# Spreading the steps of two routings and one channel attention over the slots of a hand-planned order, in a three-layer float32 network kernel

## The chip, the cores and the metric

The kernel runs on one NeuronCore of a Trainium2 chip, in one launch. The metric is the device time of that launch in microseconds (us); less is better. Names of engines: PE is TensorE (matrix products), DVE is VectorE, ACT is ScalarE, POOL is GpSimd, SP is SyncE, which starts the transfers.

## What is computed

`x` is 4 batches of 512 tokens with 128 features, in float32. Four layers follow, each adding to `x`, each behind a layer norm:

```
x = x + channel_attention(layernorm(x))   # "A": RMS norm, q k v, 8 heads, softmax(q k^T) over channels
x = x + moe_ffn(layernorm(x))             # "F": router softmax over 8 experts, a small net picks how many
x = x + token_attention(layernorm(x))     # "B": 512x512 scores, banded multipliers, softmax
x = x + moe_ffn(layernorm(x))             # "F" again, the same weights

def moe_ffn(h):
    probs = softmax(h @ router.T)                                  # 8 experts
    k     = argmax(gelu(h @ w1.T + b1) @ w2.T + b2) + 1            # 1 to 6
    score = where(rank(probs) < k, probs, 0)
    return sum_e score[e] * (silu(h @ gate[e].T) * (h @ up[e].T)) @ down[e].T
```

All eight experts are computed for all tokens; the score multiplies their hidden values.

## The kernel before, in words

**Chunks and slots.** The hidden units of the 8 experts (8 x 336) lie as 21 chunks of 128. A feed-forward layer over one batch of 512 tokens is a block of 21 chunks; there are 4 batches and 2 such layers, so 8 blocks and 168 chunks, numbered k = 0 to 167. One slot of the plan is one chunk. In each slot PE makes the gate and the up product of chunk k. Each is three matmuls of 128x512 (a high and a low part of both operands, `three`, L1112 to L1114), into PSUM banks of which gate and up have two each: gate k waits for the silu of chunk k-2, up k waits for DVE's product of chunk k-2. ACT makes `silu` of the gate (L758, step `gu`). DVE multiplies the up bank with it, or with the broadcast scores `sbc` (L1053, step `uk`). POOL multiplies the missing factor in (L635, step `um`). PE then makes the down product from SBUF (step `down`, L1297, two instructions in plain float32). From chunk 121 on, a down may be split like gate and up: ACT writes a high part (`ah`, L768), DVE a low part (`al`, L1061), and PE runs three matmuls in place of the plain product. In the first three blocks `um` multiplies by `sbc`, so a block's ums and downs can't start before its routing is done. 16 buffers `t2` lie between `uk` and `down`.

**Everything else is fitted in between.** The other layers and the routing of each block are chains of steps. Step lists (`A1_STEPS`, `F0_STEPS`, `F1_STEPS`, `F_STEPS`, `B_STEPS`, L88 to L105) give each step a due slot counted from the start of its chain; `A_STARTS` and `B_STARTS` give starts. `plan()` walks the slots. In each it puts first `gu` and `uk`, then the halves `ah`/`al` (`halves`), then up to two ums and downs (`products`), then the due steps of the chains, in a fixed order of chains. A step whose inputs are not yet planned moves its whole chain one slot later; a chain may also be moved once because the costs in `COST` would overfill ACT or DVE in that slot. Last come, every third slot, two `pieces`: ACT copies and POOL differences that split the next gate and up weights into high and low parts (L729, L619). Each engine then executes its part of this one list strictly in order, so that list is the schedule, and all waits between engines are semaphores.

**The steps of a routing.** `stats` (DVE), `rstd` (POOL, a power, L578), `xn` (ACT, four instructions, L655), `xT` (PE transposes, ACT copy to `xhF`), `xl` (DVE, low part, L907), `route` (PE, ACT), `inner` 0 and 1 (POOL, L604 and L607), `rt` (PE, DVE), `rexp` (ACT Exp, L732), `rsum` (DVE: sum, reciprocal, `pr` L1002, and the two comparisons `gt` L1006 and `ge` L1007 of each probability with the 7 others), `rrank` (DVE: `ge` times a triangle L1011, the maximum with `gt` L1013, the sum L1014), `tanh` (ACT), `gelu` (DVE L1019), `act` (PE, 8 small matmuls, L1233), `actk` (DVE, seven small instructions, L1027 to L1037), `sx` (POOL, L600), `sbc` (PE transposes L1241, ACT copy).

**The steps of a channel attention.** `asim` (PE), `ass` (DVE), `apow` (POOL L590), `ascale` (DVE: `qn`, `simT`, L940 and L941), `asT` (PE transpose L1180), `amax` (DVE L950, L953), `aexp` (ACT Exp L706), `awo` (DVE L961, L963), `am`, `am2` (PE and ACT), `y` (PE; DVE adds to X). The token attention has `bs` (PE scores), `bsp` (DVE, the bands, L1071 to L1088), `bexp` (ACT Exp L788), `bpT` (PE transposes L1327), `bo`, `bw`, `byx`.

Exp and Silu need different activation tables on ACT; each change shows as an ACT_TABLE_LOAD.

Of the kernel before, what the change touches and what calls it, by code (L numbers as in the profile page):

```python
# [56 lines left out]
WCH = 3  # L57
# [29 lines left out]
           (11, "asT"), (12, "amax"), (13, "aexp"), (14, "awo"), (16, "am"), (17, "am2"), (19, "y")]  # L87
A1_STEPS = [(2, "asim"), (3, "ass"), (3, "apow"), (4, "ascale"), (7, "asT"), (7, "amax"), (8, "aexp"), (9, "awo"),  # L88
            (11, "am"), (12, "am2"), (14, "y")]
F0_STEPS = [(0, "route"), (1, "inner", 0), (1, "rt"), (2, "rexp"), (3, "inner", 1), (4, "rsum"), (5, "rrank"), (5, "tanh"),  # L90
            (6, "gelu"), (8, "act"), (8, "actk"), (9, "sx"), (11, "sbc")]
F1_STEPS = [(0, "stats"), (0, "rstd"), (0, "xn"), (3, "xT"), (4, "xl"), (6, "route"), (7, "inner", 0), (8, "rt"), (9, "rexp"),
            (9, "inner", 1), (9, "rsum"), (11, "rrank"), (11, "tanh"), (11, "gelu"), (13, "act"),
            (13, "actk"), (14, "sx"), (16, "sbc")]
ROUTED_LATE = (0, 1, 2)
# [7 lines left out]
F_STEPS = [(0, "stats"), (1, "rstd"), (2, "xn"), (4, "xT"), (5, "xl"), (6, "route"), (7, "inner", 0), (8, "rt"), (9, "rexp"),  # L103
           (10, "inner", 1), (11, "rsum"), (12, "rrank"), (12, "tanh"), (13, "gelu"), (15, "act"),
           (15, "actk"), (16, "sx"), (18, "sbc")]  # L105
A_STARTS = (6, 24)
B_STARTS = (29, 48, 67, 90)
# [10 lines left out]
FREED_BY = dict(asim="ascale", asT="amax", act="actk")  # L118

POOL_COST = dict(wp=1.2, wd=1.2, wc=1.5, um=1.4, rstd=1.4, apow=.8, bqkl=1.4, sx=1.1, inner=1)  # L120
COST = dict(stats=(0, 0, 1.2), xn=(0, 1.2, 0), xT=(.4, .5, 0), xl=(0, 0, .6), ag=(.9, .3, 0), ar=(.5, .4, .4),
            asim=(.7, 0, 0), ass=(0, 0, .1), ascale=(0, 0, .3), asT=(.1, 0, 0), amax=(0, 0, .5), aexp=(0, 3, 0),
            awo=(0, 0, .5), am=(.3, .3, 0), am2=(.3, .3, 0), y=(.9, 0, .6), route=(.7, 1.1, 0), rt=(.4, 0, .4), rexp=(0, 2.7, 0),
            rsum=(0, 0, 1.3), rrank=(0, 0, 1.1), tanh=(0, .5, 0), gelu=(0, 0, .6), act=(.9, 0, 0), actk=(0, 0, 1.3),
            sbc=(.4, .5, 0), yT=(.4, 0, .6), bqk=(.7, 1, 0), bs=(.7, 0, 0), bsp=(0, 0, 1.2),
# [3 lines left out]
COST |= dict(ah=(0, .6, 0), al=(0, 0, .9))  # L129
DVE_LOAD = dict(uk=.7, al=.9, stats=1.4, xl=.7, ar=.6, ascale=.5, amax=.6, awo=.5, y=.7, yT=.7, rt=.8, rsum=3.6, rrank=2.9,  # L130
                gelu=1.7, actk=1.6, bv=.7, bsp=1.2, byx=2.4)
# [40 lines left out]
def plan():  # L172
# [12 lines left out]
    debt = [0.0, 0.0]  # L185
    pool_free = [0.0]
    um_end, downs, block_end = [], [0], []
    split, seen = [], [0]
    dve_load = [0.0]
    slot_of = {}  # L190
# [85 lines left out]
    while k < last - 1:  # L276
        n = (k + 1) // CH
        if (k + 1) % CH or (("xl", "F", n) if n in ROUTED_LATE else ("sbc", n)) in done:
            k += 1
            add(("gu", k))  # L280
            assert k < NT2 or ("down", k - NT2) in done
            add(("uk", k))
        else:
            for th in threads:
                th[0] -= th[0] <= k
        halves(k)
        products(k, 2)
        if wds and k >= WD_FROM and k % 2:
            add(wds.pop(0))
            debt[0] += 0.5  # L290
        pe = 2.2
        act, dve = debt[0] + 0.6, debt[1] + 0.7
        for th in threads:
            while th[1] and th[0] + th[1][0][0] <= k:
                s = th[1][0][1]
                cost = COST.get(s[0], (0, 0, 0))
                room = pe + cost[0] + DEBT
                late = (th[2] < SHIFTS
                        and (act + cost[1] > room + (cost[1] > 2) * 3 or dve + cost[2] > room))
                if not ready(s) or late:  # L300
                    th[0] += 1
                    th[2] += 1
                    break
                th[1].pop(0)
                add(s)
                pe, act, dve = pe + cost[0], act + cost[1], dve + cost[2]
        if pieces and k % WCH == 0:
            add(pieces.pop(0))
            add(pieces.pop(0))
        debt = [max(0.0, act - pe), max(0.0, dve - pe)]  # L310
        dve_load[0] = max(0.0, dve_load[0] - pe)
# [11 lines left out]
def build(nc, x_d, small_d, gate_d, up_d, down_d, w2_d, cols_d, rows_d, out_d):  # L323
# [17 lines left out]
    with ExitStack() as ctx:  # L341
# [487 lines left out]
        def _(dve):  # L829
# [16 lines left out]
            for s in steps:  # L846
# [148 lines left out]
                if kind == "rsum":  # L995
# [6 lines left out]
                    chain(dve.tensor_tensor(pr[:, :, :], pe_[:, :, :], p4[:, 2].unsqueeze(2).to_broadcast([P, NT, E]), ALU.mult))  # L1002

                    other = pr[:, :, :].unsqueeze(2).to_broadcast([P, NT, E, E])
# [3 lines left out]
                if kind == "rrank":  # L1008
                    n = s[1]
                    dve.wait_ge(pr_ready, n + 1)  # L1010
                    chain(dve.tensor_tensor(ge[:, :, :, :], ge[:, :, :, :],  # L1011
                                            tri[:, :, :].unsqueeze(1).to_broadcast([P, NT, E, E]), ALU.mult))
                    chain(dve.tensor_tensor(gt[:, :, :, :], gt[:, :, :, :], ge[:, :, :, :], ALU.max))  # L1013
                    chain(dve.tensor_reduce(rk[:, :, :], gt[:, :, :, :], AX_X, ALU.add))  # L1014
# [406 lines left out]
```

## Time and profile before

| | us |
|---|---|
| median of 3 runs | 498.91 (497.41 to 499.11) |
| the profiled execution | 500.59 |
| its span, first to last instruction | 498.5 |
| PE busy | 480.8 (96%) |
| DVE busy | 310.0 (62%) |
| ACT busy | 262.7 (53%) |
| POOL busy | 311.1 (62%) |
| mean granted TensorE clock | 0.990 |

The page divides the span in 40 slices and gives each engine's busy share there, and the clock that TensorE was granted. Beside it, the trace was asked for the waits of PE by stretch, for the timeline of single engines, and for sums over chosen windows. In a timeline, a number in square brackets is how long the engine had been idle before that instruction, and what ended it.

### The profile page before, as it was taken

What the parts mean: (1) busy time and instruction counts of PE and PEld (TensorE: products, weight loads), DVE (VectorE), ACT (ScalarE), POOL (GpSimd) and SP (SyncE); (2) the same over time, 40 slices, a digit from 0 to 9 for tenths busy, and PEclk for the clock granted to TensorE, in tenths of its full rate; (3) what the DMA queues carried; (4) which work ended last, traced back from release to release, by engine and by line L of the source; (5) the groups of instructions that cost most, each with busy time, mean ns of one, the idle gap of its engine ahead of it and who ended that gap; (6) DMA issues with size and microseconds to landing.
All of it is one profiled execution on the core that took longest, in us unless ns stands there. A gap on an engine that the chain in (4) does not pass through costs nothing.

```text
span 498.5 us, 6470 instructions
## 1 busy us (share of the span) xinstructions
PE 480.8 (96%) x2036; PEld 343.5 (69%) x2036; DVE 310.0 (62%) x723; ACT 262.7 (53%) x477; POOL 311.1 (62%) x314
## 2 busy tenths in 40 slices
PE   7898889999999897999999999999999999999997
PEld 7776756677666565576676666667666767778886
DVE  3655434735867746288855984659766466748563
ACT  3495635656714684228762559334773456345551
POOL 5365788429868284445653555557675677759774
PEclk9998899999999998999999999999999999999999
DMA  8700000000000000000000000000000000000000
GB/s 238 239 0 2 0 0 2 0 1 1 1 1 1 1 0 0 1 1 2 0 1 0 1 1 1 1 0 1 22 0 1 1 14 9 0 1 0 24 0 21
DMA packets 7933, 7.36 MB, mean 15 GB/s; under 512 B 732, under 2 KB 7772, under 8 KB 7900
## 3 DMA queue, kind: packets, MB, share of 16 engines
q1 hardware_dynamic: 7900, 6.96, 4.6%
q8 instruction: 16, 0.26, 0.2%
q14 instruction: 17, 0.14, 0.1%
HBM read 5.91 MB, written 1.05 MB: 14 GB/s over the span
## 4 chain that ended last, share of the span: by engine, by line
PE 76%; ACT 3%; DVE 2%; issue 2%; POOL 1%; ACTq 0%; POOLq 0%; DVEq 0%
PE bank L1297 19%; PE bank L1112 16%; PE bank L1114 15%; PE bank L1113 15%; PE bank L1335 3%; PE bank L1233 1%; POOL t L635 1%; PE bank L1327 1%; ACT L758 1%; PE bank L1135 1%; PE bank L1347 1%; DVE t L1053 1%; PE bank L1305 1%; PE bank L1241 1%; PE bank L1275 1%
## 5 line engine op out<-in xcount | busy, mean ns | idle before, releaser
L635 POOL TENSOR_TENSOR t<-t,sl 128x512 f32<-128x512 f32 x105 | 148.5, 1418 | 98.0 <-DVE t L1053 81.0
L758 ACT ACTIVATE sl<-bank 128x512 f32<-128x512 f32 x168 | 99.4, 596 | 135.4 <-PE bank L1114 127.1
L1297 PE MATMUL bank<-t,WD 128*128 128x512 f32 x262 | 130.3, 595 | 0.0
L1053 DVE TENSOR_TENSOR t<-bank,sbc 128x512 f32<-128x512 f32 x105 | 72.3, 689 | 64.8 <-PE bank L1114 63.4
L635 POOL TENSOR_TENSOR t<-t,sbc 128x512 f32<-128x512 f32 x63 | 80.9, 1313 | 20.0 <-DVE t L1053 11.1
L1112 PE MATMUL bank<-xhF,WGh 128*128 128x512 f32 x167 | 90.3, 541 | 1.6 <-ACT sl L758 1.6
L1053 DVE TENSOR_TENSOR t<-bank,sl 128x512 f32<-128x512 f32 x63 | 43.1, 685 | 66.4 <-PE bank L1114 27.7
L1112 PE MATMUL bank<-xhF,WUh 128*128 128x512 f32 x168 | 67.3, 401 | 1.7 <-DVE t L1053 1.7
L1114 PE MATMUL bank<-xhF,WUl 128*128 128x512 f32 x168 | 67.1, 400 | 0.0
L1113 PE MATMUL bank<-xlF,WUh 128*128 128x512 f32 x168 | 67.0, 399 | 0.0
L1114 PE MATMUL bank<-xhF,WGl 128*128 128x512 f32 x167 | 66.7, 399 | 0.0
L1113 PE MATMUL bank<-xlF,WGh 128*128 128x512 f32 x167 | 66.4, 398 | 0.0
L1297 PEld LDWEIGHTS bank<-t,WD 128*128 128x128 f32 x262 | 49.7, 190 | 21.9 <-issue 11.5
L1112 PEld LDWEIGHTS bank<-xhF,WGh 128*128 128x128 f32 x167 | 31.9, 191 | 17.4 <-issue 11.0
L1113 PEld LDWEIGHTS bank<-xlF,WGh 128*128 128x128 f32 x167 | 31.9, 191 | 14.2 <-issue 11.3
L1112 PEld LDWEIGHTS bank<-xhF,WUh 128*128 128x128 f32 x168 | 32.0, 190 | 10.3 <-DVE t L1053 2.8
L1114 PEld LDWEIGHTS bank<-xhF,WUl 128*128 128x128 f32 x168 | 32.0, 190 | 7.7
L1113 PEld LDWEIGHTS bank<-xlF,WUh 128*128 128x128 f32 x168 | 32.0, 190 | 7.5
L1114 PEld LDWEIGHTS bank<-xhF,WGl 128*128 128x128 f32 x167 | 31.7, 190 | 7.5
L758 ACT ACT_TABLE_LOAD x19 | 24.4, 1283 | 0.3
L1061 DVE TENSOR_TENSOR t2r<-t,ah 128x512 fp32r<-128x512 f32 x33 | 23.8, 722 | 0.0
L768 ACT ACTIVATE ah<-t 128x512 fp32r<-128x512 f32 x33 | 20.6, 624 | 3.3 <-POOL t L635 2.4
(209 smaller groups left out, 700.7 us busy)
## 6 DMA issues: line engine op xcount, KB each, us to landing
stage<-in_gate SPq DMA_DIRECT2D x7, 192.0 KB, 6.2
stage<-in_up SPq DMA_DIRECT2D x7, 192.0 KB, 6.3
WD<-in_down SPq DMA_DIRECT2D x7, 192.0 KB, 6.2
X<-in_x SPq DMA_DIRECT2D x4, 256.0 KB, 5.8
out<-X SPq DMA_DIRECT2D x3, 256.0 KB, 2.3
raw<-in_small SPq DMA_DIRECT2D x1, 384.0 KB, 4.9
out<-X SPq DMA_DIRECT2D x2, 128.0 KB, 1.9
raw<-in_small SPq DMA_DIRECT2D x1, 192.0 KB, 2.6
```

The costliest lines, as they stand in the source:

```text
L635: pool.tensor_tensor(t2[k % NT2][:, :], t2[k % NT2][:, :], by[:, :], ALU.mult).then_inc(a_done, 1)
L758: act.activation(sl[k % NSL][:, :], bank[k % 2][:, :], ACT.Silu).then_inc(silu_done, 1)
L768: act.activation(ah[i % NAH][:, :], t2[k % NT2][:, :], ACT.Copy).then_inc(ah_done, 1)
L1053: dve.tensor_tensor(t2[k % NT2][:, :], bank[2 + k % 2][:, :], by[:, :], ALU.mult).then_inc(t2_done, 1)
L1061: dve.tensor_tensor(t2r[k % NT2][:, :], t2[k % NT2][:, :], ah[i % NAH][:, :].bitcast(F32), ALU.subtract).then_inc(al_done, 1)
L1112: pe.matmul(out, lh, rh, start=start, stop=False)
L1113: pe.matmul(out, lh, rl, start=False, stop=False)
L1114: return pe.matmul(out, ll, rh, start=False, stop=stop)
L1135: r = pe.transpose(to[:, i * P:i * P + P], xn[:, i, :], ident[:, :])
L1233: r = pe.matmul(m[:, 8 * i:8 * i + KMAX], hq[:, i * P:i * P + P], w2[:, 0:KMAX], start=True, stop=True)
L1297: r = pe.matmul(OACC[:, :], WD[:, c, :], t2[k % NT2][:, :], start=(c == 0), stop=(c == CH - 1 or k == TAIL[0] - 1))
L1335: r = pe.matmul(m[:, :], xnB[b % 2][:, j, :], PT[:, j, :], start=(j == 0), stop=(j == NT - 1))
```

## The change

Only the order of instructions changes: the same instructions run on the same data.

- `F0_STEPS`, `F1_STEPS` and `A1_STEPS` get new due slots. The first routing's last step `sbc` is due in slot 8 in place of 11, the second's 13 slots after its chain's start in place of 16, the second batch's channel attention ends in slot 11 in place of 14. Most steps stand one slot apart.
- `rsum` is cut in two planned steps, `rsum` (softmax) and `rcmp` (the two comparisons); `rrank` too, into `rrank` (the product with the triangle) and `rmax` (maximum and sum). `F_STEPS` places the four in slots 11, 12, 13, 14.
- The third batch's channel attention starts in slot 7 in place of 6.
- Steps in `AHEAD` (`rstd`, `apow`, `sx`, `xl`, `ascale`, `amax`) that come next in their chain and are due are put right behind `gu` and `uk` of the slot, ahead of the halves, the ums and the downs and of other chains' steps.
- The two pieces that fell every third slot may wait for a slot in which ACT has room by the planner's costs.

```diff
-A1_STEPS = [(2, "asim"), (3, "ass"), (3, "apow"), (4, "ascale"), (7, "asT"), (7, "amax"), (8, "aexp"), (9, "awo"),
-            (11, "am"), (12, "am2"), (14, "y")]
-F0_STEPS = [(0, "route"), (1, "inner", 0), (1, "rt"), (2, "rexp"), (3, "inner", 1), (4, "rsum"), (5, "rrank"), (5, "tanh"),
-            (6, "gelu"), (8, "act"), (8, "actk"), (9, "sx"), (11, "sbc")]
-F1_STEPS = [(0, "stats"), (0, "rstd"), (0, "xn"), (3, "xT"), (4, "xl"), (6, "route"), (7, "inner", 0), (8, "rt"), (9, "rexp"),
-            (9, "inner", 1), (9, "rsum"), (11, "rrank"), (11, "tanh"), (11, "gelu"), (13, "act"),
-            (13, "actk"), (14, "sx"), (16, "sbc")]
+A1_STEPS = [(1, "asim"), (2, "ass"), (3, "apow"), (4, "ascale"), (5, "asT"), (6, "amax"), (7, "aexp"), (8, "awo"),
+            (9, "am"), (10, "am2"), (11, "y")]
+F0_STEPS = [(0, "route"), (1, "inner", 0), (1, "rt"), (2, "rexp"), (2, "inner", 1), (3, "rsum"), (3, "tanh"), (4, "rcmp"),
+            (4, "gelu"), (5, "rrank"), (5, "act"), (6, "rmax"), (6, "actk"), (7, "sx"), (8, "sbc")]
+F1_STEPS = [(0, "stats"), (1, "rstd"), (2, "xn"), (3, "xT"), (4, "xl"), (5, "route"), (6, "inner", 0), (6, "rt"), (7, "rexp"),
+            (7, "inner", 1), (8, "rsum"), (8, "tanh"), (9, "rcmp"), (9, "gelu"), (10, "rrank"), (10, "act"), (11, "rmax"),
+            (11, "actk"), (12, "sx"), (13, "sbc")]
...
-           (10, "inner", 1), (11, "rsum"), (12, "rrank"), (12, "tanh"), (13, "gelu"), (15, "act"),
+           (10, "inner", 1), (11, "rsum"), (12, "tanh"), (12, "rcmp"), (13, "gelu"), (13, "rrank"), (14, "rmax"), (15, "act"),
...
-A_STARTS = (6, 24)
+A_STARTS = (7, 24)
...
+AHEAD = ("rstd", "apow", "sx", "xl", "ascale", "amax")
...
-            rsum=(0, 0, 1.3), rrank=(0, 0, 1.1), tanh=(0, .5, 0), gelu=(0, 0, .6), act=(.9, 0, 0), actk=(0, 0, 1.3),
+            rsum=(0, 0, .9), rcmp=(0, 0, 1.2), rrank=(0, 0, .5), rmax=(0, 0, 1.2), tanh=(0, .5, 0), gelu=(0, 0, .6), act=(.9, 0, 0), actk=(0, 0, 1.3),
...
+        for th in threads:
+            while th[1] and th[0] + th[1][0][0] <= k and th[1][0][1][0] in AHEAD and ready(th[1][0][1]):
+                s = th[1].pop(0)[1]
+                add(s)
+                debt[0] += COST.get(s[0], (0, 0, 0))[1]
+                debt[1] += COST.get(s[0], (0, 0, 0))[2]
         halves(k)
         products(k, 2)
...
-        if pieces and k % WCH == 0:
+        owed += 2 * (k % WCH == 0)
+        while pieces and owed and act < pe + 0.8:
             add(pieces.pop(0))
-            add(pieces.pop(0))
+            owed -= 1
+            act += 0.5
...
-
+                if kind == "rcmp":
                     other = pr[:, :, :].unsqueeze(2).to_broadcast([P, NT, E, E])
                     own = pr[:, :, :].unsqueeze(3).to_broadcast([P, NT, E, E])
...
+                if kind == "rmax":
                     chain(dve.tensor_tensor(gt[:, :, :, :], gt[:, :, :, :], ge[:, :, :, :], ALU.max))
```

## Rows read from the trace of the kernel before

**Rows 1.** The page: shares of the chain that ended last, by engine.
```profile
PE 76%; ACT 3%; DVE 2%; issue 2%; POOL 1%; ACTq 0%; POOLq 0%; DVEq 0%
```

**Rows 2.** PE's waits from 36 to 75 us: us in total, times, longest.
```profile
PE bank L1112 <- DVE t L1053: 1.7, 2, 1.4
PE bank L1112 <- ACT sl L758: 1.6, 1, 1.6
PE bank L1180 <- DVE simT L941: 1.0, 1, 1.0
PE bank L1135 <- ACT xn L655: 0.4, 1, 0.4
...
```

**Rows 3.** PE's waits from 160 to 200 us.
```profile
PE bank L1327 <- DVE xlS L907: 2.5, 1, 2.5
PE bank L1112 <- DVE xlF L907: 1.6, 1, 1.6
PE bank L1112 <- DVE bmp L1085: 0.5, 1, 0.5
```

**Rows 4.** PE's waits from 300 to 412 us.
```profile
PE bank L1135 <- ACT PT L796: 0.5, 1, 0.5
PE bank L1135 <- ACT xn L655: 0.3, 1, 0.3
...
```

**Rows 5.** Windows: stretch, length, busy us of each engine, granted clock, DMA.
```profile
42.00:44.00 2.00, 2.00 (x7) 1.52 (x6) 1.76 (x10) 0.60 (x1) 1.82 (x4) 0.50 0.00 0
75.00:160.00 85.00, 85.00 (x352) 58.66 (x351) 53.50 (x133) 45.14 (x81) 59.12 (x60) 1.00 0.00 1
191.00:198.00 7.00, 4.48 (x14) 2.86 (x14) 4.22 (x7) 1.79 (x3) 3.46 (x3) 0.76 0.00 0
```

**Rows 6.** Timeline of DVE, 33 to 45 us: start, us, instruction, idle before.
```profile
35.40 0.68 DVE L1053 TENSOR_TENSOR t<-bank,sl 128x512 f32<-128x512 f32 x1
36.31 1.09 DVE L1013 TENSOR_TENSOR gt<-gt,ge 128x256 bf16<-128x256 bf16 x1
38.45 0.67 DVE L1053 TENSOR_TENSOR t<-bank,sl 128x512 f32<-128x512 f32 x1
42.05 0.17 DVE L1027 SCALAR_TENSOR_TENSOR al__95<-bank,rows 128x24 f32<-128x24 f32 x1
43.34 0.19 DVE L1037 SCALAR_TENSOR_TENSOR rk<-rk,p 128x32 f32<-128x32 f32 x1
```

**Rows 7.** Timeline of PE, 30 to 56 us.
```profile
43.12 0.63 PE L1113 MATMUL bank<-xlF,WUh 128*128 128x512 f32 x1
43.55 0.63 PE L1114 MATMUL bank<-xhF,WUl 128*128 128x512 f32 x1
46.69 0.40 PE L1113 MATMUL bank<-xlF,WUh 128*128 128x512 f32 x1
46.92 0.39 PE L1114 MATMUL bank<-xhF,WUl 128*128 128x512 f32 x1
```

**Rows 8.** Timeline of ACT, 44 to 52 us.
```profile
44.95 1.28 ACT L706 ACT_TABLE_LOAD   x1
46.64 1.63 ACT L655 ACTIVATE xn<-X,nmr,rstd 128x128 f32<-128x128 f32 x4
49.12 1.28 ACT L758 ACT_TABLE_LOAD   x1
50.41 1.08 ACT L758 ACTIVATE sl<-bank 128x512 f32<-128x512 f32 x2
```

**Rows 9.** Groups by line (count, busy, mean ns), and one DVE line's durations (min/median/max).
```profile
L600 POOL TENSOR_TENSOR sx<-rk,pr 128x512 f32<-128x512 f32 x8 | 8.4, 1055 | 4.9 <-DVE rk L1037 4.9
L1061 DVE TENSOR_TENSOR t2r<-t,ah 128x512 fp32r<-128x512 f32 x33 | 23.8, 722 | 0.0
L1011 DVE TENSOR_TENSOR ge<-ge,tri x8: 277/282/2917, 36.0 to 429.6; 128x256 bf16<-128x256 bf16 x8
```

**Rows 10.** Chain that ended last, in order of time: start, us, what.
```profile
74.38 0.86 PE bank L1297 x2
```

More of the change, by code:

```diff
@@ L129 @@
 COST |= dict(ah=(0, .6, 0), al=(0, 0, .9))
-DVE_LOAD = dict(uk=.7, al=.9, stats=1.4, xl=.7, ar=.6, ascale=.5, amax=.6, awo=.5, y=.7, yT=.7, rt=.8, rsum=3.6, rrank=2.9,
+DVE_LOAD = dict(uk=.7, al=.9, stats=1.4, xl=.7, ar=.6, ascale=.5, amax=.6, awo=.5, y=.7, yT=.7, rt=.8, rsum=1.2, rcmp=2.2, rrank=1.0, rmax=1.5,
                 gelu=1.7, actk=1.6, bv=.7, bsp=1.2, byx=2.4)
@@ L188, in plan @@
     split, seen = [], [0]
+    owed = 0
     dve_load = [0.0]
```

## The prediction

> **What bounds the kernel now.** I read the shares of the chain first: three quarters of the time that sets the end is PE executing matmuls [rows 1]. Then windows: over 85 us, from 75 to 160, PE is busy in every microsecond at full clock while DVE and ACT are busy 66% and 59% of it [rows 5]. So most of the span is a queue of PE work that this change keeps, instruction for instruction. What an order can give back is only what PE loses. I asked for PE's waits stretch by stretch. There are three places. Early, 36 to 75 us, before most downs exist: waits of 1.7, 1.6, 1.0 and 0.4 us, 4.7 together [rows 2]. In the middle, around 168 and 193 us: 2.5, 1.6 and 0.5, together 4.6 [rows 3]. Late: 0.5 and 0.3 [rows 4]. The launch up to 24 us has waits as well, but its order, the prelude, isn't touched.
>
> A wait has a second price here. Behind the early waits the granted clock is 0.50 from 42 to 44 us [rows 5], the lower level of 1.2 GHz, and the same matmuls then start 0.43 us apart, against 0.23 at 2.4 GHz [rows 7]. Twelve matmuls of chunks 9 and 12 run so, plus some small ones: some 2.8 us by (0.43 - 0.23) for each and 0.4 for the small ones. The stretch 191 to 198 has a mean clock of 0.76 [rows 5], which is 7 x 0.24 = 1.7 us. So the pool that an order can win is 4.7 + 2.8 early, 4.6 + 1.7 in the middle, 0.8 late: 14.6 us.
>
> **Why PE waits early.** Without downs a slot is only two triples, 6 x 0.23 = 1.4 us of PE. DVE's row shows the first cause: `uk` at 35.40 and the next only at 38.45 [rows 6], because `rrank` (its maximum took 1.09) and `ascale` lie between. Up 8 has to wait for that. ACT's rows show the second: from 44.95 to 50.41, 5.5 us, ACT loads the Exp table, makes `aexp`, then 1.63 us of `xn`, then two pieces, then loads the Silu table, and only then the next `silu` [rows 8].
>
> **The change, part by part.**
>
> *First routing and second batch's channel attention, closer steps.* Walking through the planner with its costs, I get: `rsum` slot 3, `rcmp` 4, `gelu` 5 (moved by one: DVE is overfull in slot 4), `rrank` and `act` 6, `rmax` and `actk` both 7, `sx` 8, `sbc` 9; for the attention `ascale` 4, `asT` 5, `amax` 6, `aexp` 7, `awo` 8, `am` 9, `am2` 10, `y` 11; `xn` of the third batch in 10. So `aexp`, `xn` and the pieces fall apart: the 5.5 us become 1.28 + 0.6 + 1.28, about 3.2, against 2.8 us of PE work for two slots: that wait of 1.6 goes, and with it the slow stretch behind it, if nothing else stops PE there.
> But one slot between a DVE step and the PE step that reads it is less than PE's lead. PE works up to two chunks ahead of `uk`, so it reaches `asT` while DVE is still one slot behind. Laying the durations of the rows end to end, up 5 ends near 33.9 and `simT` near 35.7: a wait of 1.8 (bounds 0, if DVE catches up, and 1.9). `act` waits for `gelu`: 0.5 (0 to 1). `sbc` is the largest: behind `uk` 7 stand `rmax` (1.09 + 0.42 as a bound from the slow case) and `actk`, 1.5 from 42.05 to 43.53 [rows 6], then `sx` on POOL, 1.06 [rows 9]: 1.5 + 1.5 + 1.06 = 4.0 us, while PE has 2.0 us queued: a wait of 2.0 (0 to 3). Early handoffs: 4.3. The slow clock may come behind one of them: half of 1.4, 0.7.
>
> *The second routing.* `y` of the second batch comes in slot 11, not 15, so `stats` of this routing moves from 16 to 12 and `sbc` from 31 to 24. The ums of block 1 needn't idle from slot 28 to 32. That is POOL's time, not PE's, since 75 to 160 us shows no PE wait at all; I put it at nothing (the downs in the queue hide it). `stats`, `rstd`, `xn` no longer fall in one slot, which takes the 1.0 + 0.4 at 71 us; but `amax`, `rcmp` and `gelu` share slot 20 ahead of `act` in 21, about 3.5 us of DVE against 2.3 of PE: 1.2 lost (0 to 1.5). POOL's queue is passed by `rstd`, `apow` and `sx`, each up to 1.06 us for the um behind it; its lead of two slots covers that. SP's queue isn't touched.
> Early sum: 7.5 won, 4.3 + 0.7 + 1.2 = 6.2 paid: net gain 1.3, and I add 0.5 because in the hand-laid rows PE reaches chunk 12 at the same time as now with the `am2` and `y` work already done: 1.8 (bounds: -2 and 7.5).
>
> *The bursts of the later routings.* The wait of 2.5 at 193 us is `bpT` for a bank that `xl` of the token attention frees; `xl` stands behind all of `rsum`, `uk`, `rrank`. Now `xl` goes right behind `uk`, and `rmax` is two slots off. I take 2.5 and the 1.7 of slow clock as gone: 4.2 (bounds 0 and 4.2).
> The 1.6 + 0.5 at 168 us come from two `bexp` in the slot before `xl`. `AHEAD` does nothing there, but the first token attention starts earlier: its `stats` needs `down` 20, now in slot 28 in place of 31, so the pair of `bexp` moves from 49 to 46 or 47, and the fourth routing's `xl` stays at 50. 2.1 gone from there. New meeting: `bsp` of that attention with `rcmp` to `actk` of the third routing in slots 40 to 43, about 12.4 us of DVE against 10.6 of PE. I charge 1.3 for it (0 to 1.8) and 0.4 for `rexp` and `aexp` in neighbouring slots 37 and 38. Middle: 4.2 + 2.1 - 1.7 = 4.6.
>
> *Late.* `rstd` of the last routing stood behind an um on POOL; ahead of it, `xn` comes 1.3 to 1.7 us sooner and the 0.3 and its follower go: 0.5. The 0.5 at 310 us stays. The 33 split downs [rows 9] may become one or two more or fewer as `DVE_LOAD` is spread; a plain down is 0.86 [rows 10], a split one 3 x 0.23 = 0.69, so +-0.3: nothing.
>
> **Sum.** 1.8 + 4.6 + 0.5 = 6.9 us off the profiled execution: span 498.5 to 491.6, its time 500.59 to 493.7. That execution stands 1.7 over the median of the runs, so the median goes from 498.91 to 492.0.
>
> **A rule that speaks against it.** The durations of DVE's product with the triangle run from 277 to 2917 ns for the same shape [rows 9], the long ones while POOL multiplies. The Trainium skill, SBUF — State Buffer, "SBUF: two separate sides", says that a DVE instruction with two SBUF inputs and a POOL instruction exclude each other for the whole instruction. By that rule each piece of a cut burst meets a new um, and PE's waits would be re-dealt rather than removed: it is the first rival.
>
> **Rivals.**
> 1. *The waits are only re-dealt* (0.18). A piece of DVE work held for one um costs (2917 - 277) at worst. If two of 8 routings meet so in a slot where PE has no lead, 2 x 2.6 = 5.2 us come back: 498.91 - 6.9 + 5.2 = 497.2. For it: POOL starts its ums two slots sooner, inside the first routing. Against: over the whole trace PE feels only one such case.
> 2. *PE stands at the one-slot handoffs* (0.13), the slower side. In slots 5, 6, 9 of the empty stage and again at `act` of the second routing PE waits for DVE or POOL at the upper bounds: 1.9 + 1.0 + 3.0 + 1.5 = 7.4, and each of three waits is followed by slow clock, 3 x 1.4 = 4.2: 11.6 paid for 7.5 won. It ends slower from the point at which the middle gives back less than 4.1, as when the `bexp` pairs meet other chains: with a middle of 0 it is 498.9 + 4.1 = 503.0.
> 3. *Clean sweep* (0.17). DVE catches up through `rsum` being a slot sooner and the handoffs cost little (2 us), and nothing new meets in the middle: 14.6 - 2 = 12.6 off, 486.3.
> 4. *The list doesn't spread* (0.04): chains move by a slot when a cost or an input is missing, and bursts join again, as `rmax` and `actk` do by my walk. Then nothing moves: 499.
>
> **Numbers.** The forecast case has 0.48 and spans 489 to 496. The range takes in the sweep at its 486.3 and the re-dealt case, and leaves out most of the slower one: 486.0 to 501.5. About 0.5%, 2.5 us, is what a measurement can tell from no change: faster (below 496.4) is 0.48 + 0.17 + 0.05 of the first rival = 0.70; same 0.17; slower 0.13.
>
> **What the profile will show.** Right: no PE wait on `xlS` near 190 us and no clock below 0.9 in that stretch; ACT's time between `silu` 9 and 10 under 3.5 us; PE waits of 1 to 2 us on `simT` and on `sx` before 50 us. Wrong: PE waits on `sx` over 3 us, or clock 0.5 in the early stretch as long as now (rival 2); waits over 1 us between 75 and 160 us, which has none (rival 1); a number of split downs below 28, which would add a microsecond by itself.

## The result

The changed kernel takes 501.38 us (median of 5 runs, 500.39 to 501.95), the kernel before 497.96 (5 runs beside it, 495.95 to 499.11): a ratio of 1.007, interval 1.004 to 1.0099. It is slower by 0.7%. The forecast was 492.0. In the experiments below, an execution more than 1.5% above the fastest of its kernel is left out of the median (two of ten in e12, four of ten in e13).

The profiled execution of after took 501.61 us, with a span of 499.8; that of before 500.59, with 498.5. The execution of before stands 2.6 over the 497.96, so the two spans differ by less than the medians do. PE's share of the chain that ended last is 87%, against 76% in [rows 1], but the two can't be compared: the shares of before add up to 84%, since its chain is followed back only to 74.38 us, and that of after back to 0.72. The waits say more. PE's waits of after, from 24 to 75, from 75 to 160, from 160 to 200 and from 200 to 300 us (us in total, times, longest); the lines are those of the changed kernel, some ten further down:

```profile
PE bank L1244 <- DVE hq L1030: 3.4, 1, 3.4
PE bank L1252 <- POOL sx L610: 1.1, 1, 1.1
PE bank L1123 <- ACT sl L768: 0.6, 1, 0.6
...
PE bank L1214 <- DVE bmp L1096: 3.1, 1, 3.1
PE bank L1244 <- DVE hq L1030: 0.6, 1, 0.6
...
PE bank L1123 <- DVE xlF L917: 1.7, 1, 1.7
PE bank L1123 <- DVE bmp L1096: 0.2, 1, 0.2
...
PE bank L1123 <- DVE bmp L1096: 1.0, 1, 1.0
PE bank L1123 <- ACT sl L768: 0.9, 1, 0.9
```

(The 0.6 on `sl` stands near 32 us.) Beside [rows 2 to 4]: the waits on the burst of `rrank`, on ACT's 5.5 us and on `xlS` are gone, and so are both of the late stage. In their place stand a wait of 3.4 on `gelu`'s `hq` in the empty stage, one of 3.1 in a stretch that had none, 1.7 in the place of the 1.6 on `xlF`, and 1.9 after 200 us where before had none. L1244 is `act`, L1214 is `y`, L1123 the first product of a `gu`. Windows show the clock behind the two long waits, and last its mean from 36 to 75 us, of after and, below it, of before (stretch, length, busy time of PE, PEld, DVE, ACT, POOL, granted clock, DMA):

```profile
40.00:42.00 2.00, 2.00 (x9) 1.92 (x10) 0.28 (x2) 0.00 (x0) 0.00 (x0) 0.50 0.00 0
42.00:44.00 2.00, 2.00 (x6) 1.58 (x5) 0.00 (x0) 0.60 (x1) 0.00 (x0) 0.50 0.00 0
44.00:46.00 2.00, 2.00 (x6) 1.52 (x6) 1.47 (x5) 0.31 (x1) 0.00 (x0) 0.50 0.00 0
...
155.00:159.00 4.00, 4.00 (x12) 2.64 (x11) 2.03 (x6) 0.60 (x1) 0.00 (x0) 0.57 0.00 0
...
36.00:75.00 39.00, 34.47 (x156) 26.38 (x156) 20.58 (x58) 20.54 (x49) 26.52 (x34) 0.91 0.00 1
...
36.00:75.00 39.00, 34.20 (x150) 25.88 (x150) 18.66 (x54) 19.35 (x45) 26.81 (x34) 0.91 0.00 1
```

Six microseconds at 1.2 GHz early cost 6 x 0.5 = 3.0, and 4 x 0.43 = 1.7 follow the second wait. Over the whole stretch from 36 to 75 us the mean clock is 0.91 in both kernels, which is 39 x 0.09 = 3.5 us in each: the 2.8 that I had counted for before was too little. So the early stage loses 5.1 in waits and 3.5 to the clock, 8.6 against 4.7 + 3.5 = 8.2 before; the middle loses 0.6 + 3.1 + 1.9 + 1.9 in waits and 1.7 to the clock, 9.2 against 6.3; the late stage loses nothing, against 0.8. By these counts after is 2.5 worse; the spans say 1.3, the medians 3.4.

The first wait, on DVE, 35 to 41 us (start, us, instruction, idle before):

```profile
36.28 0.35 DVE L951 TENSOR_SCALAR simT<-bank,rs 128x128 f32<-128x128 f32 x1
36.54 0.42 DVE L1016 TENSOR_TENSOR gt<-pr 128x256 bf16<-128x256 f32 x1
36.87 1.22 DVE L1017 TENSOR_TENSOR ge<-pr 128x256 bf16<-128x256 f32 x1
38.01 1.47 DVE L1030 SCALAR_TENSOR_TENSOR hq<-hq,xa 50x512 f32<-50x512 f32 x1
39.41 0.67 DVE L1064 TENSOR_TENSOR t<-bank,sl 128x512 f32<-128x512 f32 x1
```

PE had started the last product of its queue at 35.71 and stood until 39.53. No `uk` stands between `ge` and `hq`: `rcmp` and `gelu` are in one slot. `ge` and `hq` are as long as they are while POOL makes the residues of two pieces (shown by e7). The second wait, on DVE and PE:

```profile
149.23 0.17 DVE L1038 SCALAR_TENSOR_TENSOR al__95<-bank,rows 128x24 f32<-128x24 f32 x1
...
150.62 0.68 DVE L1086 SCALAR_TENSOR_TENSOR mk<-bank,mk 128x512 bf16<-128x512 f32 x1
...
153.27 0.68 DVE L1096 CUSTOM_DVE_ANT_0 Sb<-mk,bank 128x512 f32<-128x512 bf16 x1
...
154.11 1.13 PE L1214 MATMUL bank<-mixw,xaT 128*128 128x128 f32 x8 [3.07 <-DVE bmp L1096]
```

`y` of the fourth batch has all its data. What it lacks is a PSUM bank: the turns go round, and its turn falls on the bank that `bs` filled three turns earlier, which the last of four `bsp` reads out at 153.3. Before the change the steps stood in another order: its bank was that of `act`, which `actk` read out, and that work ends on DVE at 150.7 here.

### The profile page after: what moved, and what is told of

It reads as the page before. It is cut to its first block, busy times and chain, and to the rows that moved or that the text cites. A ratio compares the mean times of both kernels' runs of the same rounds, so it can differ in the third digit from the quotient of the medians.

```text
span 499.8 us, 6479 instructions
## 1 busy us (share of the span) xinstructions
PE 479.1 (96%) x2037; PEld 342.9 (69%) x2037; DVE 316.0 (63%) x724; ACT 259.7 (52%) x476; POOL 309.6 (62%) x314
## 4 chain that ended last, share of the span: by engine, by line
PE 87%; DVE 6%; ACT 3%; issue 2%; POOL 1%; DMA 1%; DVEq 0%; ACTq 0%; POOLq 0%
PE bank L1308 21%; PE bank L1123 18%; PE bank L1125 17%; PE bank L1124 17%; PE bank L1346 3%; PE bank L1244 2%; PE bank L1146 1%; PE bank L1338 1%; DVE t L1064 1%; PE bank L1358 1%; PE bank L1214 1%; PE bank L1252 1%; ACT L768 1%; PE bank L1163 1%; DMA X<-in_x 1%
## 5 line engine op out<-in xcount | busy, mean ns | idle before, releaser
L1123 PE MATMUL bank<-xhF,WGh 128*128 128x512 f32 x167 | 90.1, 540 | 1.5 <-ACT sl L768 1.5
L1123 PE MATMUL bank<-xhF,WUh 128*128 128x512 f32 x168 | 67.2, 400 | 0.0
L1123 PEld LDWEIGHTS bank<-xhF,WGh 128*128 128x128 f32 x167 | 31.9, 191 | 17.3 <-issue 11.1
L1123 PEld LDWEIGHTS bank<-xhF,WUh 128*128 128x128 f32 x168 | 32.0, 191 | 8.1 <-DVE t L1064 0.5
L1072 DVE TENSOR_TENSOR t2r<-t,ah 128x512 fp32r<-128x512 f32 x34 | 27.7, 816 | 0.0
L610 POOL TENSOR_TENSOR sx<-rk,pr 128x512 f32<-128x512 f32 x8 | 8.4, 1052 | 26.8 <-DVE rk L1048 26.8
```

Source lines behind the costliest of these rows:

```text
L610: pool.tensor_tensor(sx[:, :, :, :], rk[:, :, :].unsqueeze(3).to_broadcast([P, NT, E, P // E]), pr[:, :, :].unsqueeze(3).to_broadcast([P, ...
L1072: dve.tensor_tensor(t2r[k % NT2][:, :], t2[k % NT2][:, :], ah[i % NAH][:, :].bitcast(F32), ALU.subtract).then_inc(al_done, 1)
L1123: pe.matmul(out, lh, rh, start=start, stop=False)
```

## The experiments

Each time is a median with its range; before was run beside every group, at 498.75 to 499.11 in the median of 16 to 20 runs. "after" is 501.38. The ranges hold all executions.

| run | built on | edit | us | range |
|---|---|---|---|---|
| e1_early | after | old later routings, no steps ahead | 507.93 | 507.42-511.38 |
| e2_rest | after | old early part | 496.56 | 493.88-498.3 |
| e3_act_later | after | `act` to `sbc` of routing 1 a slot later | 500.08 | 498.29-502.91 |
| e4_b_later | after | token attention starts in slot 32 | 494.10 | 493.13-495.04 |
| e5_both | after | e3 and e4 | 488.88 | 488.83-489.54 |
| e6_bank | after | `act` ahead of the first `bs` | 496.98 | 496.57-499.43 |
| e7_pieces | after | two pieces later | 499.93 | 499.32-505.42 |
| e8_three | e5 | second routing's `act` later too | 488.35 | 488.25-488.7 |
| e9_clear | e8 | e7's edit | 487.74 | 487.71-487.94 |
| e10_old_bursts | e8 | old later routings, no steps ahead | 504.70 | 501.0-506.13 |
| e11_start29 | e8 | token attention early, e6's edit | 494.12 | 493.47-494.67 |
| e12_no_ahead | e8 | no steps ahead | 499.89 | 495.91-506.58 |
| e13_attn_ahead | e8 | only `ascale`, `amax` ahead | 497.11 | 494.25-505.59 |
| e14_rest_ahead | e8 | all but these two ahead | 493.75 | 493.67-495.77 |
| e15_half_ums | e12 | first twelve ums half as wide | 500.93 | 497.95-502.3 |
| e16_bursts_back | e8 | bursts as before | 488.71 | 488.45-488.91 |

**First cut: which half is it?** e1 keeps the new lists of the first two routings and the attention, e2 keeps the steps ahead and the broken bursts. The new rule for the pieces stands in e1 and the old one in e2; both put the pieces in the same slots, so it separates nothing.

```diff
 e1:
-AHEAD = ("rstd", "apow", "sx", "xl", "ascale", "amax")
+AHEAD = ()
-           (11, "rsum"), (12, "tanh"), (12, "rcmp"), (13, "gelu"), (13, "rrank"), (14, "rmax"),
+           (11, "rsum"), (11, "rcmp"), (12, "rrank"), (12, "rmax"), (12, "tanh"), (13, "gelu"),
 e2: A1_STEPS, F0_STEPS, F1_STEPS, A_STARTS and the costs of the first two routings as before
```

> Half of the change alone: the new A1_STEPS, F0_STEPS, F1_STEPS, A_STARTS and the split step names, with AHEAD empty, the pieces as before and F_STEPS as before (rcmp with rsum, rmax with rrank). If the closer steps of the first routings are what makes the changed kernel slower (theory of the handoffs), this one loses what the changed one loses before 60 us: PE waits 3 to 4 us for gelu's result (the changed kernel: 3.4) and about 1 us for sx, with clock 0.5 behind it, and it keeps the late wait behind rstd (0.5 to 0.9): 502 to 505 us. If the later routings cause it (rival), it is at 497 to 500.

> The other half alone: AHEAD, the new F_STEPS and the new placing of pieces, with A1, F0, F1 steps and A_STARTS as before; rcmp goes with rsum and rmax with rrank in the first two routings, at the planner costs of before. Theory: the 2.5 us wait for xlS near 193 us with its slow clock (1.7) and the late 0.9 go, nothing is paid early (same 4.7 us of waits and 2.8 of slow clock as before): 498 - 5 = 493, faster by 1%. Rival, that moved steps only re-deal the waits: new waits of 3 to 5 us elsewhere between 75 and 300 us, 497 to 499.

507.93 and 496.56. Both signs were right, both sizes off: the early part alone costs 9 us, against the 3 to 6 expected, and the rest brings 2.5 (ratio 0.9958, 0.9934 to 0.9983), against 5. In e2 the rival holds in part: the wait on `xlS` is gone, as expected, but its trace has two new ones, 1.6 on `simT` at 75 us and 2.0 at 140 us. After is 6.5 better than its early part alone, so the parts aren't additive; what the second one does for the first is taken up with e10 and e12.

**Two corrections.** e3 gives `gelu` the slot back, e4 starts the first token attention where it started before the change (its `stats` then stands in slot 32, as before, not in 31; its first `bs` in 44, where before had 43 and after 42).

```diff
 e3:
-            (5, "rrank"), (5, "act"), (6, "rmax"), (6, "actk"), (7, "sx"), (8, "sbc")]
+            (5, "rrank"), (6, "rmax"), (6, "act"), (7, "actk"), (8, "sx"), (9, "sbc")]
 e4:
-B_STARTS = (29, 48, 67, 90)
+B_STARTS = (32, 48, 67, 90)
```

> The changed kernel with act, actk, sx and sbc of the first routing one slot later. If PE's 3.4 us wait there is its lead over DVE at a one-slot handoff, one more slot gives it a gate and an up, 1.4 us, to do: the wait falls to about 2.0, and the slow clock behind it (10 matmuls 0.2 late) shortens or goes: 1.4 to 3.4 us off the changed kernel, 498 to 500 us. If DVE's own backlog sets it (rival), PE waits for uk instead by the same amount and the time stays at 501.

> The changed kernel with the start of the first token attention (B_STARTS) at slot 32 in place of 29, so that its first scores bs take their PSUM bank after act of the third routing, as in the kernel before. Theory: y of the fourth batch waits 3.1 us at 154 us only because its bank is three turns after that of bs, which four DVE steps must free; with the old order of turns the wait goes and the slow clock behind it (2.2 us): 5 us off the changed kernel, 496. Rival, that DVE's pile of bsp and routing steps in these slots is the bound: uk comes late instead and 3 us or more stay, 500 to 501.

> The changed kernel with both single corrections: the first routing's act, actk, sx and sbc one slot later, and the second batch's first attention starting in slot 32, as before the change, in place of 29. Theory (early handoff and middle bank wait are independent losses): the wait for hq near 39 us falls from 3.5 to about 1.2 and the slow clock behind it goes (worth 1.4 to 3.4 us off the 494.1 of the kernel with the later start alone), and the wait of 3.1 for a PSUM bank near 150 us stays away: 490.5 to 492.5. Rival (the early loss was hidden by something later, as its own run at 500.1 against 501.4 for the change could say): 494, no better than the later start alone.

e3 brings 1.3, e4 7.3, and both 12.5. e4 and e5 went further than I expected. PE's waits of e3 from 140 to 200 us tell why e3 alone brings so little:

```profile
PE bank L1214 <- DVE bmp L1096: 3.0, 1, 3.0
PE bank L1123 <- DVE xlF L917: 2.6, 1, 2.6
```

Early it wins 2.2 of the wait on `hq` and all of the slow clock (1.00 in each window from 40 to 46 us). Then PE comes to the same DVE work sooner and waits 2.6 instead of 1.7 there, and behind it the mean clock is 0.91 from 170 to 190 us, 1.8 us lost, where after has 1.00. From 24 us on this trace has 12.2 us of waits, against 12.6 in after. With the middle mended the early gain stays. In e5, from 24 to 75 us:

```profile
PE bank L1244 <- DVE hq L1030: 1.2, 1, 1.2
PE bank L1123 <- ACT sl L768: 0.6, 1, 0.6
PE bank L1191 <- DVE simT L951: 0.6, 1, 0.6
PE bank L1197 <- issue: 0.5, 1, 0.5
PE bank L1252 <- POOL sx L610: 0.3, 1, 0.3
```

and between 150 and 200 us it has no wait of PE at all. The traces give the 12.5 as well: from 24 us on after has 12.6 us of waits and loses 3.5 + 1.7 to the clock; e5 has 5.2 of waits and full clock in those stretches, 12.6 less.

**Bank or DVE?** In e6 DVE and POOL keep their order. Only PE's order changes, and with it whose bank falls to `y`.

```diff
+    steps.remove(("act", 2))
+    steps.insert(steps.index(("bs", 0, 0)), ("act", 2))
```

> The changed kernel, with act of the third routing put ahead of the first score product bs.0.0 in PE's order. DVE and POOL do the same steps in the same order; only the turns of the PSUM banks change, so that y of the fourth batch gets the bank that actk has read, as before the change, and not the one that bsp's last product holds. Bank theory: the wait of 3.1 at 154 us and the slow clock of about 2.2 us behind it go, 496 to 497. Rival (DVE is simply late there, so whoever reads next waits as long): a wait of 2 to 3 us for another product in 150 to 157 us, and 500 to 502.

496.98: the bank theory's number. PE's waits of e6 from 150 to 200 us are the two that after also has there, 1.7 and 0.2, and between 75 and 150 only 0.9 is left, on `hq`. So 4.4 of the 7.3 that e4 gave is one bank's turn: 3.1 of wait and most of its clock.

e11 asks what is left with the bank in order and the early part mended, when only the early start of the token attention remains (the start of e4 put back, the edit of e6 added).

> As e8_three, but the second batch's first attention starts as in the changed kernel (slot 29, in fact 31), and act of the third routing stands ahead of bs.0.0, so that the bank turn of y is the harmless one. It takes the 7.3 us that the later start gave apart: what is left above e8_three is the meeting of that attention with the third and fourth routing on DVE, without the bank. From the changed kernel: the wait of 1.7 to 2.6 for route.3's xlF and 1.0 near 217 us stay, so 488.35 + 2.5 to 4.0 = 491 to 492.4. Rival (all of it was the bank): within 1 us of e8_three, 489.

494.12, more than the 491 to 492.4 expected: 5.8 over e8. Its PE waits from 150 to 200 and from 200 to 300 us:

```profile
PE bank L1125 <- DVE xlF L919: 2.6, 1, 2.6
...
PE bank L1125 <- DVE bmp L1098: 1.0, 1, 1.0
PE bank L1125 <- ACT sl L770: 0.9, 1, 0.9
```

The first is a gate product that waits for `xl` of the fourth routing, made at 167.61 behind a `bsp` and a `stats` of the token attention; e8 has neither it nor the 1.0. The meeting on DVE that I charged with 1.3 costs up to 5.8, of which 1.6 is slow clock behind the 2.6 (a mean of 0.92 from 170 to 190 us).

**POOL beside `ge` and `gelu`.** e7 moves two pieces out of the slot.

```diff
+    for j in (12, 13):
+        steps.remove(("wp", j))
+    at = steps.index(("uk", 8)) + 1
+    steps[at:at] = [("wp", 12), ("wp", 13)]
```

> The changed kernel with two of POOL's pieces (wp 12 and 13) moved out of slot 6 to behind uk 8, so that POOL multiplies nothing while DVE makes ge and hq of the first routing. Contention theory: ge back from 1.22 to about 0.42 us and the gelu step's 1.47 to about 0.7, so PE's wait for hq falls from 3.4 to about 1.9, and some of the slow clock goes: 498.5 to 500. Rival (the DVE operations are long for another reason, or act would wait for something else): the wait stays at 3 or more and the time at 501.

DVE in e7, the lines of the same operations:

```profile
36.61 0.42 DVE L1021 TENSOR_TENSOR ge<-pr 128x256 bf16<-128x256 f32 x1
36.95 0.68 DVE L1034 SCALAR_TENSOR_TENSOR hq<-hq,xa 50x512 f32<-50x512 f32 x1
```

1.22 and 1.47 have become 0.42 and 0.68: the contention is shown. 499.93, as expected in the range; of the 1.6 us that `hq` comes sooner the wait for `sx` takes back 1.4 (1.1 became 2.5), so the 1.5 won is hardly in the waits. It is in the clock of this trace: a mean of 0.96 from 36 to 75 us in place of 0.91, 1.9 us. e9 does the same on the best kernel so far.

> The kernel with both later starts and the later second routing (e8_three, 488.35), with the two pieces of POOL moved out of slot 6 as well. There ge and the gelu step still take 1.24 and 1.48 us and PE still waits 1.2 us for hq. Contention theory: ge 0.42 and gelu 0.7, the wait for hq goes; since in the changed kernel 1.6 us of that wait came back as a longer wait for sx, here at most 1.2 is won: 487.2 to 488.3. Rival: the pieces, now behind uk 8, meet the DVE operations of slots 8 and 9 and the wait for sx (0.4) grows to 1.5 or more: 488.4 to 489.5.

487.74, 0.6 below e8; the wait for `hq` of 1.2 is gone and that for `sx` is 1.3 in place of 0.4.

e8 gives the second routing the slot as well (`act` 11, `actk` 12, `sx` 13, `sbc` 14).

> As e5_both, and also act, actk, sx and sbc of the second routing one slot later, with its rmax. Theory: the wait of 0.6 to 1.5 for hq of the second routing near 85 us goes too, and nothing is due behind its sbc, whose ums have slack: 0.5 to 1.5 below e5_both, about 490. Rival: sbc is now late for the ums of block 1 and the time is given back there as a wait for silu's or sx's results between 85 and 110 us: equal to e5_both or up to 2 above it.

488.35 against 488.88: the wait of 0.8 on `hq` near 80 us goes and nothing is given back. The rival falls.

**What are the bursts worth, and the steps ahead?** On e8, e10 takes both away, e12 the steps ahead alone, e16 the broken bursts alone (`AHEAD = ()`, and the `F_STEPS` line of e1).

> As e8_three, but the other routings with their steps as before the change (rsum and rcmp in one slot, rrank and rmax in the next) and no step put ahead of the ums: only the early part is new. It says what the bursts broken up are worth when the early part is right. My prediction's terms for them: the wait for xlS and the slow clock behind it 4.2, late 0.5, so 488.35 + 4.7 = 493, with a PE wait of 1.5 us or more on xlS or xlF between 150 and 240 us. Rival (the waits of the middle hang on where the chains meet, which moves with the early part, not on the bursts): within 1.5 us of e8_three, 488 to 490.

> As e8_three, but no step is put ahead of the ums of its slot (rstd, apow, sx, xl, ascale, amax stand in their old place in the slot). Theory: this part alone is worth the 0.5 of the late stage and at most 1.5 in the middle, where xl stands behind uk's neighbours: 488.8 to 490.3. Rival: it is worth nothing, 488.3, or the steps put ahead cost an um on POOL its time, then 487.5.

> As e8_three, with rsum and rcmp of the later routings in one slot and rrank and rmax in the next, as before the change; the steps put ahead stay ahead. My prediction had 4.2 us for xlS near 193 us here, but the waits of the kernel without both parts are at each place those of the kernel without the steps ahead alone: within 1 us of e8_three, 488 to 489. By the prediction's term: 492 to 493 with a wait on xlS of 1.5 or more.

504.70, 499.89 and 488.71. e10 and e12 missed all their ranges, by 9.6 us and more. With the steps ahead in place the bursts broken up are worth 0.4 us, hardly more than the ranges (e16). Without the steps ahead the medians of e10 and e12 lie 4.8 apart, and the traces don't say why: the two profiled executions have the same waits and nearly the same time. The steps ahead are worth 11.5 with the bursts broken, where I had 0.5 late and a share of the 4.2 on `xlS`. The executions of e12 and of e13 below differ by 11 us among themselves, and the profiled one of e12 took 504.58, so its lines show the dear case; e10, profiled at 504.74 and so at its own median, has the same three waits (3.5, 4.2 and 4.0). e12 from 24 to 75, from 75 to 150 and from 200 to 300 us:

```profile
PE bank L1191 <- DVE simT L951: 3.4, 1, 3.4
...
PE bank L1123 <- DVE t L1064: 4.2, 1, 4.2
...
PE bank L1123 <- ACT sl L768: 4.1, 3, 3.3
```

e13 and e14 take the group apart.

```diff
 e13:
+AHEAD = ("ascale", "amax")
 e14:
+AHEAD = ("rstd", "apow", "sx", "xl")
```

> As e8_three (488.35), but only ascale and amax of the channel attention are put ahead; rstd, apow, sx and xl stand in their old place. If the 12 us lie in the attention's short chain (simT 2.8 us sooner near 37 us, amax ahead of uk near 84): 488.5 to 491, with no wait on simT over 1 us and pr under 2 us. Rival (they lie in POOL's and xl's steps): 496 to 500, with the waits of 4 us near 84 and 230 us still there.

> As e8_three, but only rstd, apow, sx and xl are put ahead, ascale and amax are not. By the first theory: the wait on simT of 3.4 near 38 us is back (2.8 and perhaps the slow clock), and where the wait of 4.2 near 84 hangs on amax too: 492 to 499. By the rival: 489 to 491, only the early wait.

497.11 and 493.75. e13 is its rival's number, 8.8 us over e8 for the steps of POOL and `xl`; e14 is 5.4 over e8 for the two of the attention, inside the first theory's range. By the waits the rival is right there: in e14 the wait of 3.5 on `simT` is back and the two later ones aren't; in e13 it is the reverse (0.6 on `simT`, then 3.6 and 3.9). Which of the four steps mends the two later waits wasn't taken apart. `ascale` stands ahead of `rcmp` and `gelu` on DVE where it is put ahead, behind them where it isn't.

The 4.2 us near 84 us stand behind an odd instruction. DVE in e12, and POOL beside it:

```profile
77.77 7.60 DVE L1012 TENSOR_TENSOR pr<-pe__88,p 128x32 f32<-128x32 f32 x1
...
74.17 11.16 POOL L645 TENSOR_TENSOR t<-t,sbc 128x512 f32<-128x512 f32 x9
```

The same instruction takes 0.191 us at its shortest in that kernel. It ended when POOL's row of nine ums ended (85.37 and 85.33), as it did in e10 (84.09 and 84.04) and e13 (82.51 and 82.45). e15 makes the first twelve ums half as wide; the second half of those products is left out.

```diff
-                    pool.tensor_tensor(t2[k % NT2][:, :], t2[k % NT2][:, :], by[:, :], ALU.mult)
+                    w = 256 if k < 12 else 512
+                    pool.tensor_tensor(t2[k % NT2][:, :w], t2[k % NT2][:, :w], by[:, :w], ALU.mult)
```

> As e12_no_ahead (500.68), but the ums of the first twelve chunks multiply only the first half of their columns (the second half of those products is left out), so POOL's nine multiplications in a row near 75 to 85 us are shorter. Theory (pr, 0.2 us of work, takes 7.6 us because POOL's row of ums holds DVE): pr falls below 3 us, PE's wait of 4.2 near 84 us goes, the rest stays: 4 to 6 us less, 495 to 497. Rival (pr is late for another reason): pr stays over 6 us and the time at 500 to 501.

`pr` took 1.11 us and the wait of 4.2 went, as the theory has it, and the time stayed at 500.93, as its rival has it. But the edit missed its target: by 75 us the first eleven ums are done, so in the row beside `pr` only the first of nine is half as wide. The row is 11.07 us long, against 11.16, and eight full ums make up most of it (`pr`; the row; POOL from 76 to 85.5 us):

```profile
79.51 1.11 DVE L1013 TENSOR_TENSOR pr<-pe__88,p 128x32 f32<-128x32 f32 x1
...
74.83 11.07 POOL L646 TENSOR_TENSOR t<-t,sbc 128x256 f32<-128x256 f32 x9
...
L646 POOL TENSOR_TENSOR t<-t,sbc 128x512 f32<-128x512 f32 x8 | 10.4, 1328 | 0.0
```

So the width of the ums was not tested, and a row of nine doesn't always hold `pr` to its end. That the time stayed is partly the clock's doing. Up to 48 us the two kernels do the same with the same wait of 3.4 on `simT`, yet the slow stretch behind it was short in e12 (first three lines) and long in e15:

```profile
40.00:42.00 2.00, 2.00 (x6) 1.22 (x4) 0.00 (x0) 0.60 (x1) 0.39 (x1) 0.50 0.00 0
42.00:44.00 2.00, 2.00 (x12) 1.73 (x12) 1.60 (x4) 0.00 (x0) 0.00 (x0) 0.85 0.00 0
44.00:46.00 2.00, 2.00 (x10) 1.60 (x9) 1.26 (x5) 1.64 (x2) 0.00 (x0) 1.00 0.01 4
```

```profile
40.00:42.00 2.00, 2.00 (x6) 1.55 (x6) 0.41 (x2) 0.59 (x1) 0.73 (x2) 0.50 0.00 0
42.00:44.00 2.00, 2.00 (x9) 1.42 (x7) 1.22 (x3) 0.01 (x1) 0.00 (x0) 0.50 0.00 0
44.00:46.00 2.00, 2.00 (x7) 1.69 (x7) 0.73 (x3) 0.00 (x0) 0.00 (x0) 0.50 0.00 0
46.00:48.00 2.00, 2.00 (x7) 1.52 (x6) 0.65 (x2) 1.90 (x3) 0.00 (x0) 0.50 0.02 4
```

That is 2 x (0.50 + 0.15) = 1.3 us in e12 and 4 x 1.0 = 4.0 in e15, 2.7 us given back by the clock. In e10, behind the same wait (3.5), there was none, and in e16 there was some behind a wait of 1.2 (first line e10, then e16):

```profile
40.00:48.00 8.00, 7.71 (x41) 5.98 (x40) 5.90 (x23) 5.46 (x11) 2.02 (x5) 1.00 0.00 1
...
40.00:42.00 2.00, 2.00 (x9) 1.70 (x9) 1.90 (x7) 0.00 (x0) 0.49 (x2) 0.65 0.00 0
42.00:44.00 2.00, 2.00 (x6) 1.52 (x6) 0.80 (x3) 1.95 (x3) 0.00 (x0) 0.50 0.01 4
```

So the price of one and the same wait changes from execution to execution, and the 4.2 us of this one trace are not to be read off the medians. Why `pr` is held, and what it costs in the median, is open, since each kernel has one trace. e10 (7.59) and e13 (6.76) show it too, e8 and e14 don't (0.54 and 1.38).

## Why the prediction was wrong

The time of 501.38 lay at the far end of the range, and the sign was wrong. By the steps of the prediction:

- **What bounds the kernel** was right. Two readings for it were wrong, with no effect on the sum: the row for 75 to 160 us has DVE busy 53.50 of 85 us and ACT 45.14, 63% and 53%, not 66% and 59%; and the 76% of [rows 1] are shares of a chain followed through 84% of the span. The pool of 14.6 us was a fair count, with the early clock 0.7 short: the best kernel wins 11.1 of it (498.86 to 487.74).
- **The walk through the planner** went wrong first. I had `rsum` in slot 3, `rcmp` in 4 and `gelu` in 5. In the list that `plan()` of the changed kernel returns, the chain moves by one slot already at `inner` 1, which uses up the one move that the planner allows it for its costs; `rsum` comes in 4, and `rcmp` and `gelu` both in 5, with `act` in 6. In the middle I had the token attention two or three slots sooner; it comes one slot sooner (`stats` in 31, not 32).
- **The early handoffs** failed, in place and in size. I had 1.8 on `simT`, 0.5 on `gelu`, 2.0 on `sx`. Measured: none listed, 3.4, 1.1. The sums, 4.3 and 4.5, agree by luck. `simT` is in time because `ascale` is one of the steps put ahead, which I didn't carry into the walk; without that its wait is 3.4 (e12). `gelu` is late since it stands behind `rcmp` in its slot, which the walk had a slot apart, and both ran beside POOL's two pieces: 0.80 + 0.79 us more than in e7. I had the row that warns of it, 277 to 2917 ns for one shape [rows 9], and used it for a rival only.
- **The slow clock** was the term that turned the early sign. I took 2.8 as won and half of 1.4 as paid; by the traces 3.5 is lost in either kernel, so nothing was won. In after, the wait of 3.4 was followed by six microseconds at 1.2 GHz. So the early net was +1.8 in the sum and by the traces is -0.4. Part of this is luck of the execution: behind early waits of 3.2 to 3.5 the mean clock from 36 to 75 us was 1.00 in e10, 0.96 in e4, e12 and e14, 0.91 in after, e1 and e6, 0.87 in e15, a loss of 0 to 5.1 us. With no early wait over 1.2 it was 1.00 in e3, e5, e8, e11 and e13, but 0.96 in e16; and before itself lost its 3.5 behind waits of at most 1.6.
- **The second routing**: I charged 1.2 at its `act`; 0.6 in the trace of after, and mending it is worth 0.5 (e8). Right in kind, half the size.
- **`xlS` at 193 us** is gone with its slow clock (1.00 from 191 to 198). The effect was right; the reason isn't needed: the wait stays away with the bursts back together (e16), and also with no step ahead (e10 and e1, which have neither). The plan of every kernel with the new early part has this `xl` in slot 54; before had it in 57, in the slot of the `bpT` that needs its bank. In e2 it stands in 57 still and the wait is gone as well, so there the steps ahead and the broken bursts do what I forecast. With the steps ahead in place, breaking the bursts up is worth 0.4, not 4.2.
- **The 168 us waits** I counted as gone since the token attention starts sooner. The plan moves the pair of `bexp` only from slot 49 to 48, not to 46 or 47, with `xl` in 50 as before, and 1.7 + 0.2 of the 2.1 comes back, the 1.7 on the same `xl`, now behind a `bsp` and a `stats` of the token attention on DVE.
- **The pile on DVE** in slots 40 to 43 was seen, and charged with 1.3 (0 to 1.8) by comparing DVE's total with PE's. Two things were missing: a PSUM bank held by the last link of the `bsp` chain, which stops a `y` that has nothing to do with that chain (4.4, e6), and the shift of that pile into the fourth routing (up to 5.8 with the rest of the meeting, e11). This is the step that failed most: the middle was +4.6 in the sum and -2.9 by the traces.
- **Steps put ahead** I had at 0.5, late, and with the bursts at 4.2. They are worth 11.5 where the rest is mended (e12). With the broken bursts they keep after 6.5 below e1's 507.93; how the two share that wasn't measured.
- **Late**: the two waits are gone, 0.8 against my 0.5. One more down is split, 34 in place of 33, within what I allowed.

The second rival had the sign and was nearest in time (503.0), but its mechanism, three early waits at their bounds and a middle that gives nothing, is half of what happened: one long early wait, and a middle that costs. The sign I had named for the first rival, waits over 1 us between 75 and 160 us, is there too; its cause, DVE held by POOL, isn't what made the 3.1.

Both losses are small edits away. e9, with four steps of either of the first routings a slot later, the token attention where it was and two pieces moved, takes 487.74 against 498.86 beside it: ratio 0.9767, interval 0.9736 to 0.9799. Some 3 of these 11.1 us are clock: the fastest execution of before in that group, at a mean clock of 1.000, took 495.79, 8.1 more than the fastest of e9, also at 1.000. PE's share of e9's chain:

```profile
PE 92%; ACT 3%; DVE 2%; POOL 1%; issue 1%; DMA 1%; DVEq 0%; ACTq 0%; POOLq 0%
```

## What to carry to other kernels

When steps move in a hand-ordered schedule, follow the PSUM banks as well as the data: a product waits for whoever reads out the bank its turn falls on, and that can be a chain it shares nothing with. Price a wait by the clock behind it, too, and as a range: 3.2 to 3.5 us in one piece cost 0 to 5.1 us more here, waits up to 1.2 mostly nothing and once 1.6. Run the planner in place of walking it, since one slot missed put `rcmp` and `gelu` together here. And test a bundle by taking single parts out of the mended version: two losses of 1.3 and 7.3, alone, were worth 12.5 together, since part of a gain ahead of an unmended wait is waited away there.

## What was not expected of the hardware

- A DVE instruction with two SBUF inputs may be held not for one POOL instruction but for a row of them: 0.19 us of work took 7.60 us beside a row of nine ums (e12), 7.59 in e10 and 6.76 in e13. Beside other rows of ums the like of it gets its turn after one or two of them (`ge` 1.49, `hq` 1.78 in e8), and so did `pr` (1.11) beside a row of nine in e15. What decides between the two isn't shown. The Trainium skill, SBUF — State Buffer, "SBUF: two separate sides", has each of the two hold the shared ports for its whole instruction; the 1.22 and 1.47 of after against 0.42 and 0.68 in e7 agree with that, and the 7.60 goes beyond what it says.
- One and the same wait on `simT` was followed by no loss to the clock in one execution (e10, 3.5), by 1.3 us in another (e12, 3.4) and by 4.0 in a third (e15, 3.4), between 40 and 48 us.
- Executions of one kernel lie apart by amounts that change with the order of its work: 0.23 us in e9 and 0.45 in e8, 11 us in e12 and e13, 5 us in before. The kernels that lie within 0.8 us are those without a PE wait over 1.3 us behind the launch (e5, e8, e9, e16, with four executions each). In before the granted clock goes with the time: 495.8 to 496.0 us at 0.999 to 1.000, 500.5 to 500.7 at 0.990 (16 executions). That the waits cause the spread isn't shown.
